# Four kinds of 128x128 transposes moved from TensorE to VectorE, DMAs and GpSimd, in a kernel of turns

## The reference

```python
L0: relu((A@x + b_in)*sig(x@w_in + ..) + (A@x + b_out)*sig(x@w_out + ..) + x*sig(x@w_loop))
L1: batchnorm(relu(batchnorm((Ahat@x)@W1.T + b1))@W2.T + b2)       # statistics over all batches
L2: Wh = x@W;  e = leaky(s1[:,:,None] + s2[:,None,:]), masked where adj == 0;  softmax(e)@Wh
L3: h = relu(A@(x@Wg0 + bg0)); h = relu(A@(h@Wg1 + bg1))
    for p in 1..4: run an LSTM over windows of p nodes of h; write its last state into the window's last node
```

## Time and profile before

| | |
|---|---|
| time, median of 3 runs | 638.07 us |
| the profiled execution: its time, its span | 637.48, 635.7 us |
| busy in the span: PE, DVE, ACT, POOL | 621.7, 469.7, 433.1, 168.9 us |
| the stretch before turn 2 | 0 to 188.45 us |
| turns 2 to 7 | 57.2 and five times 57.4 us |
| turns 8, 9 | 50.7, 52.2 us |
| DMA traffic | 16.84 MB, nearly all before 62 us and the stores of `out` |

### The profile page before, as it was taken

The page is one execution under the profiler, slowest core; times in us unless marked ns, Lnnn a source line. Parts: engine busy times, 40 slices in busy tenths (PEclk is TensorE's granted clock), DMA queues, the critical chain, the costliest instruction groups (busy, mean ns, idle before and its releaser), DMA issues.

```text
span 635.7 us, 9580 instructions
## 1 busy us (share of the span) xinstructions
PE 621.7 (98%) x2768; PEld 441.7 (69%) x2768; DVE 469.7 (74%) x1623; ACT 433.1 (68%) x995; POOL 168.9 (27%) x228
## 2 busy tenths in 40 slices
PE   9999999999999999999999999999999999999994
PEld 6756656447975687579658766865885687577794
DVE  4999999877857657866886687588668766465656
ACT  3667767866947766785677577657847766546774
POOL 1464551005233002303603240341143032103201
PEclk9999999999999999999999999999999999999998
DMA  8334000000000000000000000000000000000000
GB/s 342 129 123 167 1 1 1 1 0 2 2 1 1 0 2 1 1 2 33 2 0 2 33 2 2 34 2 1 1 33 2 2 32 2 1 1 34 2 35 34
DMA packets 4372, 16.84 MB, mean 26 GB/s; under 512 B 480, under 2 KB 480, under 8 KB 4192
## 3 DMA queue, kind: packets, MB, share of 16 engines
q1 hardware_dynamic: 4320, 16.23, 6.6%
HBM read 12.03 MB, written 4.19 MB: 26 GB/s over the span
## 4 chain that ended last, share of the span: by engine, by line
PE 77%; DVE 3%; ACT 2%; issue 1%; POOL 0%; POOLq 0%; ACTq 0%; DVEq 0%
PE QQ L831 27%; PE QQ L843 15%; PE PA L814 4%; PE PA L786 4%; PE PB L805 2%; PE PB L796 2%; PE PB L667 2%; PE PA L667 2%; PE PB L767 2%; PE PA L767 2%; PE QQ L865 1%; PE PB L884 1%; PE PA L746 1%; PE PB L746 1%; PE QQ L875 1%; PE PA L777 1%
## 5 line engine op out<-in xcount | busy, mean ns | idle before, releaser
L1200 ACT ACTIVATE raw<-QQ,BL 128x256 f32<-128x256 f32 (+2 forms) x279 | 150.3, 559 | 78.5 <-PE QQ L843 39.9
L831 PE MATMUL QQ<-HT,WT 128*128 128x256 f32 (+2 forms) x558 | 183.5, 473 | 0.8 <-DVE HT L1708 0.4
L446 POOL TENSOR_TENSOR RSD<-VAR,pw 128x4 f32<-128x4 f32 (+1 forms) x43 | 62.0, 1443 | 379.1 <-DVE VAR L1422 379.1
L831 PEld LDWEIGHTS QQ<-HT,WT 128*128 128x128 f32 x558 | 103.9, 190 | 58.2 <-issue 29.7
L843 PE MATMUL QQ<-HB,WT 128*128 128x256 f32 (+2 forms) x336 | 100.1, 441 | 0.2
L843 PEld LDWEIGHTS QQ<-HB,WT 128*128 128x128 f32 x336 | 61.2, 190 | 28.8 <-issue 13.4
L1236 ACT ACTIVATE raw<-raw 128x256 f32<-128x256 f32 (+4 forms) x79 | 37.0, 469 | 22.8 <-DVE raw L1690 18.8
L1680 DVE SCALAR_TENSOR_TENSOR raw<-raw 128x256 f32<-128x256 f32 (+2 forms) x60 | 31.9, 532 | 22.7 <-ACT raw L1200 21.9
L1708 DVE SCALAR_TENSOR_TENSOR HB<-raw 128x256 f32<-128x256 f32 (+4 forms) x42 | 19.9, 474 | 25.1 <-ACT raw L1236 25.1
L512 POOL TENSOR_SCALAR X<-four,MEAN,RSD 128x128 f32<-128x128 f32 x64 | 32.8, 526 | 1.6
L1042 ACT ACTIVATE X<-Z,OFF,RSD 128x128 f32<-128x128 f32 x80 | 31.8, 482 | 2.0 <-POOL OFF L452 2.0
(11 more groups left out here) (249 smaller groups left out, 1173.9 us busy)
## 6 DMA issues: line engine op xcount, KB each, us to landing
four<-in_x SPq DMA_DIRECT2D x8, 512.0 KB, 3.9
raw<-in_xt SPq DMA_DIRECT2D x8, 512.0 KB, 6.3
out<-four SPq DMA_DIRECT2D x7, 512.0 KB, 2.6
WT<-in_lstm SPq DMA_DIRECT2D x1, 2048.0 KB, 9.3
later<-in_later SPq DMA_DIRECT2D x1, 725.5 KB, 10.1
AD<-in_adj SPq DMA_DIRECT2D x2, 256.0 KB, 4.6
out<-four SPq DMA_DIRECT2D x2, 256.0 KB, 2.0
early<-in_early SPq DMA_DIRECT2D x1, 275.0 KB, 4.5
```

The lines of the kernel that those rows point to most:

```text
L446: pool.tensor_tensor(RSD[kk][:, ts], VAR[kk][:, ts], pw[:, ts], ALU.pow).then_inc(ln[k]["rstd"], some)
L831: mm = pe.matmul(steps_view(Q[q], k), WT[:, 0, (p - 1) * 4 + q, :], ht_view(par, k), start=True, stop=(s == 0))
L1200: act.activation(TG[q][:, at:n], Q[q][:, at:n], ACT.Tanh, scale=0.5 if q == G else 0.25, bias=BL[:, p - 1, q:q + 1]).then_inc(g_ok, 1)
```

## The change

In turns 2 to 9 the four kinds of transposes leave PE. Three of them (`a_residual`, `t_turn`, `a_turn_e`) become: DVE transposes 32x32 blocks inside each quarter of the partitions (`y_blocks`, `t_blocks`, `e_blocks`), SP stores the 512 KB to DRAM, waits, and loads four quarters of 128 KB back so that the blocks land in the right place. The sums with x go from DVE to POOL (`y_sum`, `t_sum`). `a_rows` becomes a 128x32 block transpose at the end of `a_s12`, four small stores, and one load that spreads the row over 128 partitions (`r_through`). The scaling of the first norm goes from ACT (`norm_apply`) to POOL (`scale1`). The attention's front (`y_sum`, its statistics, `a_dots`, `a_s12`) of group s+1 now stands in turn s; batch 3 of `a_mix` and batches 2 and 3 of `a_project_mix` go to turn s+1. Each engine's order within a turn is written out anew.

```diff
 SP, new:
+def y_through(g):
+    sp.wait_ge(y_blk, g - 1)
+    sp.dma_start(turn_y[g], YD).then_inc(y_put, 16)
+    sp.wait_ge(y_put, 16 * (g - 1))
+    reach(sp, z1_ok, NC * (g - 2))
+    for q in range(P // QUAD):
+        sp.dma_start(quad_rows(YF, q), quad_source(turn_y[g], q)).then_inc(y_got, 16)
 # t_through(g) and e_through(g, h), half h of the weights, are built alike
+def r_through(g):
+    sp.wait_ge(r_blk, g - 1)
+    for q in range(P // QUAD):
+        sp.dma_start(turn_r[g]...[q], S2T[q * QUAD:q * QUAD + TILES, :]).then_inc(r_put, 16)
+    sp.wait_ge(r_put, 64 * (g - 1))
+    sp.wait_ge(max_ok, TILES * g) if g > 2 else sp.wait_ge(att_ps, GB)
+    sp.dma_start(ROWS, turn_r[g:g + 1, :].broadcast_to([P, COLS])).then_inc(r_got, 16)
+def slot(s, ...):   # t_through(s-3); y_through(s+2); e_through(s,0); e_through(s,1); r_through(s+1); store out[s-3]
 POOL, a turn:
+    rstd(2, 1, s - 1, 1); scale2(s - 1, 1); t_sum(s - 3); y_sum(s + 1); scale1(s); scaled(s + 3)
+    rstd(1, 0, s + 1); tail(s - 3, 1 - par); rstd(2, 1, s, 0); scale2(s, 0)
 PE, a turn:
+    x(0); x(1); a_project_mix(s-1, (2,)); a_mix(s-1, (3,)); a_spread0(s-1, (0, 1), 0)
+    x(2); a_project_mix(s-1, (3,)); x(3); h(3); a_spread0(s-1, (2, 3), 1); a_weigh0(s-1, 0)
+    x(4); a_weigh0(s-1, 1); x(5); h(5); x(6); a_weigh1(s-1, 0); a_weigh1(s-1, 1); h(6)
+    a_mix(s, (0,)); a_spread1(s-1); x(7); x(8); a_mix(s, (1,)); h(8)
+    x(9); a_project_mix(s, (0,)); a_project_mix(s, (1,)); h(9); x(10); a_mix(s, (2,)); h(10)
 DVE, a_max:
-    dve.wait_ge(s2_ps, halves(g, h))
+    dve.wait_ge(s2_ps, halves(g, h)) if g < 2 else dve.wait_ge(r_got, 16 * (g - 1))
 DVE, a turn:
+    a_max(s, (0,)); inner(0); a_max(s, (1,)); a_bias(s, 0); state(0)
+    a_max(s, (2,)); inner(1); a_max(s, (3,)); a_bias(s, 1); state(1)
+    t_blocks(s-3); inner(2); a_sum2_mix(s-1, (2,)); state(2); a_sum2_mix(s-1, (3,))
+    a_stats2(s-1, 1); a_small2(s-1, 1); y_blocks(s+2); inner(3); state(3); t_stats(s-3)
+    inner(4); a_biased0(s-1, 0); state(4); a_biased0(s-1, 1); e_blocks(s, (0,)); e_blocks(s, (1,))
+    inner(5); norm_small(3, 2, s-3); state(5); a_stats1(s+1, 0); a_stats1(s+1, 1)
+    a_biased1(s-1, 0); a_biased1(s-1, 1); inner(6); state(6); e_blocks(s, (2,)); e_blocks(s, (3,))
+    a_hidden(s-1, 1-par); inner(7); a_inverse(s); state(7); a_small1(s+1); a_dots(s+1, 0, 0); a_dots(s+1, 0, 1)
+    inner(8); state(8); a_dots(s+1, 1, 0); a_dots(s+1, 1, 1); a_sum2_mix(s, (0,)); a_sum2_mix(s, (1,))
+    inner(9); state(9); a_stats2(s, 0); a_small2(s, 0); a_s12(s+1); inner(10); state(10)
 DVE, before turn 2 (added among the steps of groups 0 and 1):
+    y_blocks(2) ... a_stats1(2, 0); a_stats1(2, 1); a_small1(2); ... y_blocks(3); a_sum2(0, (3,)) ...
+    a_biased1(0, 1); a_dots(2, ...) x4; a_s12(2); a_sum2(1, (3,)); a_stats2(1, 1); a_small2(1, 1)
```

More of the change, by code:

```diff
@@ L671, in _ @@
                 output1(i, h)
[L674 to L681, removed]
             def a_preload(g, h):
+                pe.wait_ge(out2_ok, 2 * (GROUPS - 1)) if g == 0 else None
                 bs = slice(2 * h, 2 * h + 2)
@@ L900, in h @@
                     lstm_h(s - 2, k) if L else None
[L902 to L919, removed]
+                if s == 2:
+                    x(0)
+                    x(1)
+                    a_spread0(s - 1, (0, 1), 0)
+                    x(2)
+                    x(3)
+                    h(3)
+                    a_spread0(s - 1, (2, 3), 1)
+                    a_weigh0(s - 1, 0)
+                    x(4)
+                    a_weigh0(s - 1, 1)
+                    x(5)
+                    h(5)
+                    x(6)
+                    a_weigh1(s - 1, 0)
+                    a_weigh1(s - 1, 1)
+                    h(6)
+                    a_mix(s, (0,))
+                    a_spread1(s - 1)
+                    x(7)
+                    x(8)
+                    a_mix(s, (1,))
+                    h(8)
+                    x(9)
+                    a_project_mix(s, (0,))
+                    a_project_mix(s, (1,))
+                    h(9)
+                    x(10)
+                    a_mix(s, (2,))
+                    h(10)
                     return
@@ L1288, in _ @@
+                state(9)
+                gate(10, I)
+                gate(10, G)
+                gate(10, F)
+                gate(10, O)
+                a_mixed(s, (2,))
+                state(10)
             act.wait_ge(bn_ok, HC + 1)
@@ L1832, in slot @@
+                a_bias(s, 1)
                 state(1)
-                a_norm1(s) if A else None
-                cell(2)
-                t_sum(s - 3) if T else None
-                if A:
-                    a_dots(s)
-                    a_s12(s)
-                cell(3)
-                a_max(s) if A else None
-                cell(4)
-                a_biased0(s - 1) if B else None
-                a_bias(s) if A else None
-                cell(5)
-                t_stats(s - 3) if T else None
@@ L1858, in slot @@
-                cell(9)
-                if A:
-                    a_norm2(s, 0)
-                    a_sum2_mix(s, (2, 3))
-                cell(10)
-                a_stats2(s, 1) if A else None
+                t_blocks(s - 3)
+                inner(2)
+                a_sum2_mix(s - 1, (2,))
+                state(2)
+                a_sum2_mix(s - 1, (3,))
+                a_stats2(s - 1, 1)
+                a_small2(s - 1, 1)
+                y_blocks(s + 2) if Y else None
+                inner(3)
@@ new lines, in slot @@
+                state(3)
+                t_stats(s - 3)
+                inner(4)
+                a_biased0(s - 1, 0)
+                state(4)
+                a_biased0(s - 1, 1)
+                e_blocks(s, (0,))
+                e_blocks(s, (1,))
+                inner(5)
+                norm_small(3, 2, s - 3)
+                state(5)
+                a_stats1(s + 1, 0) if N else None
+                a_stats1(s + 1, 1) if N else None
+                a_biased1(s - 1, 0)
+                a_biased1(s - 1, 1)
@@ new lines, in slot @@
+                inner(6)
+                state(6)
+                e_blocks(s, (2,))
+                e_blocks(s, (3,))
+                a_hidden(s - 1, 1 - par)
+                inner(7)
+                a_inverse(s)
+                state(7)
+                a_small1(s + 1) if N else None
+                a_dots(s + 1, 0, 0) if N else None
+                a_dots(s + 1, 0, 1) if N else None
+                inner(8)
+                state(8)
+                a_dots(s + 1, 1, 0) if N else None
@@ L1865, in _ @@
+                a_dots(s + 1, 1, 1) if N else None
+                a_sum2_mix(s, (0,))
+                a_sum2_mix(s, (1,))
+                inner(9)
+                state(9)
+                a_stats2(s, 0)
+                a_small2(s, 0)
+                a_s12(s + 1) if N else None
+                inner(10)
+                state(10)
             dve.memset(front(1).WH[:, :, P + 1:P + 2], 1.0).then_inc(zero_ok, 1)
```

899 lines of the change are left out of this document (705 added, 194 removed).

## The result

The changed kernel takes 676.63 us (median of 4 runs, 674.63 to 681.51) against 637.83 before: ratio 1.062, 95% interval 1.056 to 1.0679. The forecast was 650.5, the range 633 to 663: the direction was right, the size was not. The profiled execution took 674.63 us with a span of 672.8, 37.1 longer than the span before.

The account below looks back on a forecast made before the run. The prediction took PE's instruction order as the bound in turns 2 to 7. To the profiled execution's 637.48 us it added 9.0 for the stretches and turns and 4.0 for the clock, giving 650.5, range 633 to 663.

Parts of the forecast that it names:

- waits at `h(10)`: Eight a_dots and two a_sum2_mix batches delay inner(9) on DVE, so PE waits 0.7 us more per turn.
- turn 8: Turn 8 gets 1.75 us of attention and loses 0.95 of transposes: +0.8.
- What leaves PE: Four kinds of transposes leave PE, 4.45 us per turn, so PE alone would take 52.97 instead of 57.42.
- The row: Turns 2 to 7: the score row's path takes 6.4 us, then DVE 6.1; PE stands still 4.7 before x(2).
- The clock: PE's granted clock falls in the six gaps of turns 2 to 7, 0.66 us each, +4.0 in all.
- rival 1: The clock falls in every gap and comes back late, 2.65 us for each of six: 662.4 us; chance 0.12.
- POOL: POOL gains sums and scalings, some 9.4 us, reaching 25 of 58 per turn; costed at nothing.
- Rival 2: POOL becomes late through the shared SBUF interface, holding h(5) and a_mix(0), +2.7 us in five turns: 664; chance 0.11.
- The start: Before turn 2 DVE gets 8.7 us more work, so turn 2's x(0) starts 4.4 later (0 to 8.7).
- Turn 9: Turn 9 loses t_turn on its chain: -0.7 us.
- rival 3: Faster: the row's path is shorter and the row comes in time, 630 us halfway, 614 fully hidden; chance 0.15.

Follow-up runs that it names:

- e10: Changed kernel with the turn, the stretch before turn 2 and SP's sends reordered, y_sum one turn earlier, a_dots in two-tile pieces: 619.2 us, ratio 0.9714 to the kernel before.
- e15: Changed kernel with POOL's t_sum and y_sum cut to one column of each tile block, orders, waits and transfers kept: 664.3 us, ratio 1.0406 to the kernel before.
- e1: Changed kernel with the four a_max and two a_bias of a turn moved behind state(1) on DVE: 645.8 us, ratio 1.0125 to the kernel before.
- e5: Changed kernel with filler matmuls of ones on PE before x(2), 19 calls a turn, 28 in turn 2: 664.0 us, ratio 1.0428 to the kernel before.
- e14: Changed kernel with only the stretch before turn 2 reordered, the row ahead of y_through(3) on SP: 675.8 us, ratio 1.0555 to the kernel before.
- e8: e1 with the turn's order reset, the stretch before turn 2 reordered, and t_blocks of the last turn behind state(1): 649.7 us, ratio 1.0192 to the kernel before.
- e4: e1 with each of POOL's sums cut from two instructions of 512 columns into eight of 128: 649.7 us, ratio 1.0194 to the kernel before.

## Why the prediction was right and wrong

By its own steps, in us of the profiled execution, forecast and measured:

| Step | Forecast | Measured |
|---|---|---|
| before turn 2 | +4.4 | +6.7 |
| turns 2 to 7 in all | +8.5 | +27.0 |
| of these: waits before `x(2)` (idle) | 28.2 | 29.9 |
| of these: waits at `h(10)` | 3.5 | 2.2 |
| of these: clock | 4.0 | 12.3 |
| of these: `a_spread0(2, 3)` and `x(4)`, turns 3 to 7 | 0 | 8.9 |
| turn 8 | +0.8 | +1.1 |
| turn 9 | -0.7 | +2.3 |
| sum | +13.0 | +37.1 |

The lines within the turns are start to start against the usual pace of the same matmuls, except the first, which is idle time and has some 0.16 of restart on each wait.

1. **What leaves PE** was right: 52.97 forecast for a turn of PE alone, 52.89 in turn 6 of e10.
2. **The row** was right in place and size. The chain has 1.0 for the issues, 1.2 for the stores and 4.4 for the spread, 6.6 against 6.4 (the spread was 1.1 longer, the stores shorter), then 6.2 of DVE against 6.1, and 4.70 of idling in turn 5 against 4.7. That turn 5 meets the forecast to 0.01 is luck, as the idling goes with the two transfers of the row: 3.7 in turn 3, where store and spread take 4.6 together, 4.7 in turn 5 with 5.6, 5.5 in turn 6 with 6.4. Turn 2 has 6.8, and 5.4 without POOL's sums (e15). e1 confirms that it was the row.
3. **The clock** failed by its size. I took 0.66 per gap, since the gap was "not much longer" than the idle stretch of the earlier trace rows; the six gaps cost 2.05 each on average, from 1.6 in turn 5 (4.20 against 2.58) to 2.9 in turn 2. That is nearer the upper bound of 2.65 than the 0.66, and I had chosen near the lower end with nothing measured in between. (The bound rested on the pace of the first matmuls alone: the granted clock in the window from 0 to 6.4 us reads 1.00.) The rule of the Trainium skill ("TensorE: Matmul & The Clock Gate", "HAM oscillation") that I set as rival 1, that bursts behind waits pay for the halved clock each time, was the right mechanism: 0.50 behind every gap before `x(2)`, and e5 prices it at 12.6.
4. **POOL** failed as a step that I had costed at nothing. Rival 2 named the shared port but let POOL be the slower one. It was DVE that stood still, in the middle of the cell that sets `h_ok`, and in front of `x(4)` and not of `a_mix(0)`. The Trainium skill says in "SBUF — State Buffer", section "SBUF: two separate sides", that the port pair of the two engines is an exclusive lock for the whole instruction, that a DVE instruction with two SBUF inputs needs it, and that the other one fully blocks. These traces agree: 0.43 becomes 1.29 to 1.48 beside sums of some 1.4, one-input instructions keep their 0.27, and with the sums cut to pieces of 0.46 the delay is 0.26 at most in `state(3)`. The row of the kernel before shown above was there to be read. My reading of the earlier trace rows was loose as well: the 1.0 to 2.1 of the powers mixes two shapes, 1.0 to 1.5 for four columns and 1.6 to 2.1 for eight, so only part of that spread can be the sharing.
5. **The start** was 2.3 short. The wait at `a_spread0(0, (2, 3))` was in the forecast as 3.0; it is 2.4 in the trace, and what follows it runs at 1.2 GHz (granted clock 0.50 from 180.9 to 184.0; eight matmuls 3.36 from start to start against 1.73). e14 shows that the 6.7 are order: turn 2 starts at 189.05 there.
6. **Turn 9** failed in sign. I took `t_turn` off its chain, and forgot that `t_blocks` (2.02 on DVE) goes between `state(0)` and `inner(1)` there: PE waits 1.5 at `lane_x(2, 0)` for it. That alone only uses up what `t_turn` gave: up to there the turn takes 8.25 against 8.22. The 2.3 come behind it, 1.5 of them among the lane steps of 172 and 168 columns, where DVE's `t_stats` (1.64) now stands; which instruction causes them is open, though it is not the length of POOL's sum, as e15 has the same 54.5. e8 shows that the next place for `t_blocks` is no better; a good one was not found.

The range failed for a reason beyond the sizes. I treated clock and POOL as alternatives, each from the same forecast, 662.4 and 664. They do not exclude each other and came together: from 650.5 the two would have given 676. That this is the measured time is luck: the two terms came out smaller than the rivals had them (the clock 12.3 instead of 15.9, POOL 8.9 instead of 13.5), and the start, turn 9 and the row made up the rest. The mechanism of rival 3 (a shorter way of the row) did not come; what made the kernel faster in e10 was a row that nobody has to wait for, at the price of an order.

## What to carry to other kernels

Work taken off the bounding engine pays only if what replaces it stands in no in-order queue in front of that engine's next link: before counting the gain, walk each queue (DVE's, POOL's and SP's DMA issues) and ask what stands behind the instruction that now waits. A wait on TensorE is to be priced with the matmuls behind it, and a two-input POOL instruction with the two-input DVE instructions beside it. Rivals that do not exclude each other are added for the range.

## What the hardware showed that was not expected

The clock's price of a gap isn't fixed: behind about 4.7 us of idling `x(2)` took 4.20 instead of 2.58 in turn 5, and in turn 4 of e14 the clock was at its lower level for at least 5.6 us; even 2.0 of idling (e1) and 2.4 (before turn 2) brought it down. The same gap does not always do it: in e4 PE idles 2.0 before the same matmuls in turns 4 and 5, and behind it the granted clock is 0.51 in the one and 1.00 in the other:

```profile
329.10:332.60 3.50, 3.50 (x8) 2.80 (x9) 0.71 (x2) 0.15 (x1) 3.50 (x8) 0.51 0.00 0
388.20:392.00 3.80, 3.58 (x13) 2.35 (x14) 0.71 (x2) 0.75 (x2) 3.80 (x9) 1.00 0.00 0
```

Cheap matmuls of ones in the gap kept it at 1.00 (turn 5 of e5). A transpose of 32x32 blocks on DVE, not in the trace before, takes 1.24 for 1024 columns in `y_blocks`, and 1.98 in `t_blocks`, whose input has a stride; no run separates the stride from the rest. The four-kilobyte row spread to 128 partitions took 4.4 in the median (3.4 to 4.6), no less than the 3.9 of the 512 KB loads from distinct addresses. In e5 PE's 26.6 us of extra matmuls (28 and 5 x 19 calls of 0.216) made the kernel 12.6 faster: an engine kept busy for nothing cost less than the same engine idle.
